# One operand moved to PSUM, sixteen gathers issued early, the tensor engine's edge loop written out, and the slots' stores issued by the scalar engine

## What is computed

```python
# L0, attention: softmax over a node's edges, weighted sum of h[src]
e = leaky_relu(a_src[src] + a_dst[dst], 0.2)
e = exp(e - segment_max(e, dst)[dst])
out = segment_sum((e / segment_sum(e, dst)[dst])[:, :, None] * h[src], dst)
x = layernorm(x + layernorm_affine(x + out @ proj_W.T))
# L1, twice: maximum over a node's edges
msg = x[src] @ W_msg + edge_attr @ W_edge
c = leaky_relu(segment_max(msg, dst) + x @ W_root + b)
# L2, twice: mean of h[src];  L3, three times: sum of h[src] * dis[src] * dis[dst]
```

## Time and profile before

| | us |
|---|---|
| median of 3 runs (8475.9 to 8486.47) | 8480.8 |
| the profiled execution, its own time | 8488.48 |
| its span | 8486.7 |
| POOL busy | 5071.0 (60%) |
| PE busy | 5045.5 (59%) |
| DVE busy | 4849.4 (57%) |
| ACT busy | 2773.5 (33%) |

### The profile page before, as it was taken

One profiled execution on the slowest core, in us unless ns is written; L12 is line 12 of the kernel. 1 busy time (PEld: TensorE's weight loads), 2 busy tenths in 40 slices (PEclk: granted clock), 3 DMA queues, 4 the chain that ended last, 5 costly groups with the idle time before them and its releaser, 6 DMA issues.

```text
span 8486.7 us, 103142 instructions
## 1 busy us (share of the span) xinstructions
PE 5045.5 (59%) x25358; PEld 3381.7 (40%) x25358; DVE 4849.4 (57%) x11584; ACT 2773.5 (33%) x4849; POOL 5071.0 (60%) x5030
## 2 busy tenths in 40 slices
PE   2100000000026887878786778877878598999998
PEld 1000000000013343433344434433434298999998
DVE  4654444444476666666666666666666676332234
ACT  0222222222214555555554455555555300000000
POOL 6777777777735777777777677777777600000000
PEclk6555555555556556555555555555555599999999
DMA  5232222222214444444443444444444365766766
GB/s 139 79 88 78 79 77 80 77 79 78 79 25 116 130 130 130 129 131 131 131 131 104 127 130 129 129 131 130 130 130 130 95 227 206 268 213 220 267 219 238
DMA packets 604993, 1132.63 MB, mean 133 GB/s; under 512 B 165186, under 2 KB 372437, under 8 KB 604328
## 3 DMA queue, kind: packets, MB, share of 16 engines
q1 hardware_dynamic: 407622, 678.22, 24.0%
q0 software_dynamic: 159184, 251.10, 14.2%
q10 hardware_dynamic: 37906, 200.73, 6.0%
HBM read 716.84 MB, written 412.70 MB: 133 GB/s over the span
## 4 chain that ended last, share of the span: by engine, by line
POOL 57%; PE 20%; issue 18%; DVE 3%; DMA 0%; ACT 0%; DVEq 0%; POOLq 0%; SPq 0%; ACTq 0%
POOL CG L466 55%; PE psB L721 6%; PE psX L721 6%; PE psA L721 6%; PE psO L653 2%; POOL ad_starts L440 1%; POOL EG L490 1%; PE psX L644 1%; PE psO L781 0%; DVE stat L1123 0%; DVE stat L1127 0%; DVE ARENA L1145 0%; DVE X L1125 0%; DVE EG L1126 0%; DMA ARENA<-ad_starts 0%
## 5 line engine op out<-in xcount | busy, mean ns | idle before, releaser
L466 POOL DMA_INDIRECT CG<-table,BUF x4704 | 4709.1, 1001 | 1615.9 <-issue 1433.0
L698 PE MATMUL psO<-WE,BUF 32*128 32x96 f32 x6272 | 1288.0, 385 | 95.3 <-issue 78.7
L698 PEld LDWEIGHTS psO<-WE,BUF 32*128 32x128 f32 x6272 | 1208.0, 291 | 229.0 <-issue 229.0
L764 PE MATMUL psA<-ident,F 128*100 128x128 f32 x1 | 0.5, 453 | 1895.8 <-DVEq L1347 1895.8
L1435 DVE TENSOR_SCALAR BUF<-iota,EG 128x392 bf16<-128x392 f16 x3136 | 1074.7, 343 | 0.0
L453 POOL CAST CG<-EG x35 | 26.0, 742 | 1315.2 <-DVEq L1118 1315.2
L1434 DVE TENSOR_SCALAR BUF<-iota,EG 128x128 bf16<-128x128 f16 x3136 | 772.2, 246 | 19.4 <-DMA EG<-step_rows 19.4
L764 PEld LDWEIGHTS psA<-ident,F 128*100 128x100 f32 x1 | 0.2, 160 | 1896.2 <-DVEq L1347 1896.2
L963 ACT COPY psX<-BUF 128x768 f32<-128x768 f32 x392 | 314.4, 802 | 1014.4 <-DVE STG L1449 493.1
L1443 DVE TENSOR_TENSOR STG<-CG,psO 128x768 f32<-128x768 f32 x196 | 288.5, 1472 | 601.2 <-DMA CG<-table,BUF 601.2
L1372 DVE TENSOR_TENSOR terms<-CG,ARENA 128x32 f32<-128x32 f32 x196 | 42.0, 214 | 1031.4 <-DMA CG<-table,BUF 1031.3
(11 more groups left out here) (276 smaller groups left out, 7866.8 us busy)
## 6 DMA issues: line engine op xcount, KB each, us to landing
BUF<-counts SPq DMA_DIRECT2D x245, 784.0 KB, 5.8
BUF<-counts ACTq DMA_DIRECT2D x245, 784.0 KB, 6.4
counts<-BUF SPq DMA_DIRECT2D x1572, 98.0 KB
hist<-CG SPq DMA_DIRECT2D x392, 384.0 KB
hist<-CG SPq DMA_DIRECT2D x196, 416.0 KB
CG<-table,BUF POOLq DMA_INDIRECT x4704
BUF<-in_edge_attr SPq DMA_DIRECT2D x392, 128.0 KB
table<-TB SPq DMA_DIRECT2D x14, 336.0 KB
```

Of the source, the lines that this page charges most:

```text
L466: pool.indirect_dma_start(out=rows_in[:, r, k, :], out_offset=None, in_=tab, in_offset=bass.IndirectOffsetOnAxis(ap=SRC[:, u * S + k:u * S ...
L698: mm = pe.matmul(ETERM[:, s, k // 4, (k % 4) * DIM:(k % 4 + 1) * DIM], EA[:, s, k, :], WE[:, n0 // ITERS, :], start=True, stop=True)
```

## The change

1. **Weights in PSUM.** `psB` is declared earlier, and `weights` is a view of it. ACT makes two exponentials a slot in place of one: the decays as before, and the weights into PSUM. DVE's product reads the weights there. ACT takes the exponentials of slot u after slot u - 1 has been scanned, for there is one weights tile.
2. **16 early gathers.** `gather_slot(0)` stands ahead of the scatters of the start, behind a wait for the stored table, and `gather_slot(1)` behind them, ahead of the wait for the reloaded values.
3. **PE's passes written out.** The hardware loop of `edge_terms` is straight code; PE waits once a slot for all four scaled identities (`keep_ready` now counts slots), ahead of the slot's first count matmul; one-hots count steps and not tiles (DVE increments `onehot_ready` once for each four).
4. **ACT issues the stores.** `store(u - 1)` stands right behind `rows_back(u - 1)` on ACT, in all three passes; SP has none.

```diff
--- before.py
+++ after.py
@@ -122,6 +121,8 @@
     psX = ctx.enter_context(nc.psum_tensor("psX", [P, 1024], F32))
+    psB = ctx.enter_context(nc.psum_tensor("psB", [P, 512], F32))
+    weights = psB[:, 0:HEADS * K9].rearrange("p (h k) -> p h k", h=HEADS)
     X = sb("X", [P, NB, DIM])
...
@@ -433,6 +434,17 @@
+        def gather_slot(u, tab, rows_in):
+            for k in range(S):
+                pool.indirect_dma_start(
+                    out=rows_in[:, u % RING, k, :], out_offset=None, in_=tab,
+                    in_offset=bass.IndirectOffsetOnAxis(ap=SRC[:, u * S + k:u * S + k + 1], axis=0)).then_inc(
+                        gathered[u % RING], 16)
+        pool.wait_ge(edges_loaded, EDGES_LOADED)
+        pool.wait_ge(table_stored, 16 * NG)
+        gather_slot(0, table0, ROWS0)
         pool.wait_ge(node_idx, 1)
@@ -440,6 +452,7 @@
                                     bounds_check=EPAD - 1, oob_is_err=False).then_inc(ad_scattered, 16)
+        gather_slot(1, table0, ROWS0)
         pool.wait_ge(ad_stored, 16)
@@ -458,23 +471,17 @@
-            for u in range(SLOTS):
+            for u in range(2 if q == 0 else 0, SLOTS):
                 r, lap = u % RING, q * LAPS + u // RING
...
                     pool.wait_ge(hist_stored[r], 16 * lap)
-                for k in range(S):
-                    pool.indirect_dma_start(
-                        out=rows_in[:, r, k, :], out_offset=None, in_=tab,
-                        in_offset=bass.IndirectOffsetOnAxis(ap=SRC[:, u * S + k:u * S + k + 1], axis=0)).then_inc(
-                            gathered[r], 16)
+                gather_slot(u, tab, rows_in)
...
-            if q == 0:
-                pool.wait_ge(edges_loaded, EDGES_LOADED)
             pool.wait_ge(table_stored, 16 * NG * (q + 1))
...
@@ -552,15 +554,9 @@
-            def store(u):
-                r, lap = u % RING, q * LAPS + u // RING
-                sp.wait_ge(block_done[r], lap + 1)
-                sp.dma_start(rec[:, u * S * width:(u + 1) * S * width], ring[:, r, :]).then_inc(hist_stored[r], 16)
             for u in range(SLOTS):
...
                     flush(u)
-                store(u)
                 if q in MAX_PASSES and u + 2 < SLOTS:
@@ -665,40 +661,28 @@
-        def count_steps(m, i, s):
-            for j in range(CS):
-                k = m * HALF + s * CS + j
-                sums = psM[j % 2][:, 0:CW]
-                pe.wait_ge(onehot_ready, i * (2 * HOTS) + (HOTS * (m * SLOTS + s) + 4 * j + 4))
-                pe.sem_inc(turn["pe"], 1)
-                pe.wait_ge(acc_ready, i * (2 * CS) + (k + 1))
-                pe.sem_inc(turn["pe"], 1)
-                pe.matmul(sums, LO[:, j, 0, :], RHS[:, j, 0, :], start=True, stop=False)
-                pe.matmul(sums, LO[:, j, 1, :], RHS[:, j, 1, :], start=False, stop=False)
-                pe.wait_ge(keep_ready, i * (2 * CS) + (k + 1))
-                pe.sem_inc(turn["pe"], 1)
-                pe.wait_ge(acc_ready, i * (2 * CS) + (k + 2))
-                pe.sem_inc(turn["pe"], 1)
-                pe.matmul(sums, KI[:, j, :], ACC[:, (j - 1) % CS, :], start=False, stop=True).then_inc(counted, 1)
         def edge_terms(q):
...
             m = MAX_PASSES.index(q)
-            n0 = m * ITERS
             pe.wait_ge(out_used, out_group_base({1: MAX1, 2: MAX2}[q], "carry") + 1)
-            with pe.Fori(0, ITERS) as i:
-                for s in range(2):
-                    pe.wait_ge(ea_loaded[s], i * 16 + 16 * (n0 + 1))
-                    pe.sem_inc(turn["pe"], 1)
-                    pe.wait_ge(eterm_used, i * 2 + (m * SLOTS + s + 1))
-                    pe.sem_inc(turn["pe"], 1)
-                    for k in range(S):
-                        mm = pe.matmul(ETERM[:, s, k // 4, (k % 4) * DIM:(k % 4 + 1) * DIM], EA[:, s, k, :],
-                                       WE[:, n0 // ITERS, :], start=True, stop=True)
-                    mm.then_inc(eterm_ready[s], 1)
-                    count_steps(m, i, s)
+            for u in range(SLOTS):
+                s = u % 2
+                pe.wait_ge(ea_loaded[s], 16 * (m * ITERS + u // 2 + 1))
+                pe.wait_ge(eterm_used, m * SLOTS + u + 1)
+                for k in range(S):
+                    mm = pe.matmul(ETERM[:, s, k // 4, (k % 4) * DIM:(k % 4 + 1) * DIM], EA[:, s, k, :],
+                                   WE[:, m, :], start=True, stop=True)
+                mm.then_inc(eterm_ready[s], 1)
+                pe.wait_ge(keep_ready, m * SLOTS + u + 1)
+                for j in range(CS):
+                    k = m * HALF + u * CS + j
+                    sums = psM[j % 2][:, 0:CW]
+                    pe.wait_ge(onehot_ready, k + 1)
+                    pe.wait_ge(acc_ready, k + 1)
+                    pe.matmul(sums, LO[:, j, 0, :], RHS[:, j, 0, :], start=True, stop=False)
+                    pe.matmul(sums, LO[:, j, 1, :], RHS[:, j, 1, :], start=False, stop=False)
+                    pe.wait_ge(acc_ready, k + 2)
+                    pe.matmul(sums, KI[:, j, :], ACC[:, (j - 1) % CS, :], start=False, stop=True).then_inc(counted, 1)
             pe.wait_ge(acc_ready, (m + 1) * HALF + 2)
@@ -912,8 +896,9 @@
             for j in range(CS):
-                nc.scalar.activation(KI[:, j, :], ident[:, :], ACT.Copy,
-                                     scale=STEP[:, 4, u * CS + j:u * CS + j + 1]).then_inc(keep_ready, 1)
+                keep = nc.scalar.activation(KI[:, j, :], ident[:, :], ACT.Copy,
+                                            scale=STEP[:, 4, u * CS + j:u * CS + j + 1])
+            keep.then_inc(keep_ready, 1)
             for j in range(CS):
...
@@ -928,23 +915,29 @@
                                state_cols[u % 2][:, :, 1:K9].rearrange("p c k -> p k c")).then_inc(block_done[u % RING], 1)
+            def store(u):
+                act.wait_ge(block_done[u % RING], u // RING + 1)
+                act.dma_start(stored_rows[:, u * S:(u + 1) * S, :], ROWS0[:, u % RING, :, :]).then_inc(hist_stored[u % RING], 16)
...
             for u in range(SLOTS):
+                if u:
+                    act.wait_ge(scanned, u)
                 act.wait_ge(exp_in, u + 1)
-                nc.scalar.activation(EX[:, u % 2, :, :, :], EX[:, u % 2, :, :, :], ACT.Exp).then_inc(exp_done, 1)
+                nc.scalar.activation(EX[:, u % 2, 0, :, :], EX[:, u % 2, 0, :, :], ACT.Exp).then_inc(scales_made, 1)
+                nc.scalar.activation(weights, EX[:, u % 2, 1, :, :], ACT.Exp).then_inc(exp_done, 1)
                 if u + 2 < SLOTS:
                     head_resets(u + 2)
-                if u:
-                    act.wait_ge(scanned, u)
-                act.wait_ge(exp_done, u + 1)
+                act.wait_ge(scales_made, u + 1)
                 nc.scalar.copy(scales[:, :, 1:K9].rearrange("p (h w) k -> p h w k", w=HW),
...
                     rows_back(u - 1)
+                    store(u - 1)
                 c = (u - 2 - COLUMNS_SLOT) // 3
...
@@ -966,6 +962,10 @@
                                max_cols[u % 2][:, :, 1:K9].rearrange("p c k -> p k c")).then_inc(block_done[u % RING], 1)
+            def store(u):
+                act.wait_ge(block_done[u % RING], q * LAPS + u // RING + 1)
+                act.dma_start(stored_rows[:, u * S:(u + 1) * S, :], ROWSW[:, u % RING, :, :]).then_inc(hist_stored[u % RING], 16)
@@ -976,9 +976,11 @@
                     rows_back(u - 1)
+                    store(u - 1)
                 count_steps(m, u)
...
             rows_back(SLOTS - 1)
+            store(SLOTS - 1)
@@ -1392,7 +1394,7 @@
                         ROWS0[:, r, :, 0:SW].rearrange("p k (h w) -> p h w k", w=HW),
-                        EX[:, b, 1, :, 1:K9].unsqueeze(2).broadcast_to([P, HEADS, HW, S]), ALU.mult))
+                        weights[:, :, 1:K9].unsqueeze(2).broadcast_to([P, HEADS, HW, S]), ALU.mult))
                 if u:
@@ -1431,8 +1433,9 @@
                     for a in range(2):
-                        ts(LO[:, j, a, :], iota16[:, 0:P], STEP[:, 2 + a, column], None, ALU.is_equal).then_inc(onehot_ready, 1)
-                        ts(RHS[:, j, a, :], iota16[:, :], STEP[:, a, column], None, ALU.is_equal).then_inc(onehot_ready, 1)
+                        ts(LO[:, j, a, :], iota16[:, 0:P], STEP[:, 2 + a, column], None, ALU.is_equal)
+                        hot = ts(RHS[:, j, a, :], iota16[:, :], STEP[:, a, column], None, ALU.is_equal)
+                    hot.then_inc(onehot_ready, 1)
                 if u:
...
```

11 lines of the change are left out of this document (4 added, 7 removed).

## The result

The changed kernel takes **8267.8 us** (median of 4 runs, 8261.0 to 8269.8), the kernel before 8480.8 in the same comparison: ratio 0.9747, 95% interval [0.973, 0.9764]. Forecast were 8304, range 8273 to 8335. The profiled execution took 8261.0 us with a span of 8259.2.

What follows compares the result with a forecast made beforehand. POOL's row of gathers was taken to bound all three passes. Terms -161 + 1 - 17 = -177 took the profiled 8488.5 to 8311.5; with the runs' median 7.7 lower, the forecast was 8304 us, range 8273 to 8335.

Steps and rivals of the forecast that it cites:

- Weights in PSUM, -161 + 1: Pass 0: gathers beside DVE's product fall from 1.82 to 0.94 us, -161 (ends -150 and -173); last slot's exponentials +1.
- Rival A: Pass 0: something accompanying the product, not the product itself, holds the gather, which stays at 1.82; 8465 us, chance 0.04.
- half of the 23: Pass 0, first 26 slots: table pieces may catch gathers freed from the product; gain between 0 and 23, taken as 11.
- Early gathers, -17: Start: 16 gathers issued early bring slot 2 forward from 224.41; -17 us, ends -14 and -19.
- Stores on ACT, 0, by the issue: All passes: ACT's store issue, 0.5 to 0.6 us, is hidden or lies off POOL's row; 0 us.
- rival C: Passes 1 and 2: ACT's store issue takes 6.50 us and the loop outlasts POOL's slots; 8608 us, chance 0.03.
- PE's passes, 0 by cover: Passes 1 and 2: last count sum comes 1.6 us later, covered by 0.9 us of slack before the scan's end; 0.
- theory C: Passes 1 and 2, formed after the measurement: PE's wait delays flushes, so the last gather lands sooner; 16 to 18 us each.
- passes 1 and 2 as 0: Passes 1 and 2: POOL's row of gathers was to stay as before, with no gain or loss in the sum.
- a fifth of the 84 us either way: Passes 1 and 2: allowance for small phase shifts under the one-hots, widening the range from 8290 and 8318 to 8273 and 8335.
- rival B: Passes 1 and 2: late count sums shift one-hots, stretching gathers; +120 us, so 8424, or down to 8220; chance 0.07.

Runs made afterwards that it cites:

- experiment 1: The kernel before with only the product's weights moved to PSUM, ACT's two exponentials behind the scan: 10,439.3 us, ratio 0.9994, on a chip where before takes 10,410.6.

## Why the forecast was right, and where it was wrong

- **Weights in PSUM, -161 + 1: right.** -170.3 and -167.7, inside the ends, and the cause is shown (experiment 1). Rival A, 8465, is out. The 10 us more are in the slots with a table piece, for which I had taken 11, half of the 23: from slot 2 to 25 the stretched time fell by 21 us, in the 170 others by 149. The Trainium skill, SBUF - State Buffer, "Who interferes with whom", infers that a `tensor_tensor` does not stall the making of DMA descriptors. The gather, a DMA that POOL issues, is held up all the same by one with two SBUF inputs: 1.82 against 0.94 us, by that operand. Whether it is held at its reading of the row numbers, which the section's other rule would cover, or at the writing of descriptors, no run tells. That other rule I had given without its condition: the section frees a DVE instruction with one SBUF input only outside DVE's 2-port performance modes, and names `tensor_scalar`, which the one-hots are, among those that can enter them. The one-hots have one SBUF input and do stretch gathers here, by up to 0.2 us in the means above; in which mode they run no trace shows.
- **Early gathers, -17: right**, -17.1 and -17.3, and 15 to 18 in the run with them alone. The first scatter came at 115.11 (forecast 114 to 116).
- **Stores on ACT, 0, by the issue: right in size, wrong in what else it moves.** ACT's issue takes 0.33, not 0.5; rival C, which needed 5, is out. But I had counted the store that SP loses, and not the DMA that stands behind it on SP's queue, the edge load, which now goes 2 us ahead of the store. Whether that moved anything is open.
- **PE's passes, 0 by cover: right.** The first count matmul follows the identities by 0.05, not 0.6; the last sum of a slot ends 1.4 us ahead of the scan's end, so the cover held, with more left than the 0.9 forecast. Whether this part moved the phase (theory C) is open.
- **The step that failed: passes 1 and 2 as 0, with "a fifth of the 84 us either way".** I had named the 84 us of stretched gathers and their dependence on phase, and then allowed 17 us. It was 35 and 12. Of that stretched time 54 us were in the 341 gathers of phase 0.15 to 0.25, and with one-hots 0.28 us earlier six in seven of them were gone; on the second chip, with one-hots 0.21 earlier, 304 of 340 still stood there and lost 31 us in place of 55. The range for such a term should have been nearly all of it, 70 us down and as much up. In rival B I had the mechanism and its ends, 8220 to 8424, which hold the result, but gave it 7 in 100 and tied it to a late count sum; the one-hots did not come late, they came earlier. That the second chip's time lies inside the range is luck of the same kind.

What is shown: the stretching differs by the phase and the pair, and its change accounts for the time by which passes 1 and 2 fell, on both chips. What moved the phase is open. The edge load's place is supported by a correlation within the kernel before, and four slots without that load speak against it; part 3, by the later flushes, stays possible. What makes five chips take 22 to 27% longer is open as well.

## What to carry to other kernels

Where one engine's row of short, equal instructions is the bound, price each held-up instruction by the operand kind of what runs beside it: an operand moved to PSUM gave 0.88 us a slot here. When a DMA leaves a queue, look at what stood behind it there, since that now starts earlier (here by some 3 us against the last gather), and price it as a term of its own. And where two periodic rows beat against each other, the time hangs on hundredths of a us: take the whole of the stretched time as the range, and measure on more than one chip before a per cent is believed.

## What the runs showed that I had not expected

- In the kernels before and changed, on the chips where POOL is the bound, a gather that starts 0.14 to 0.21 us behind a pair of one-hots loses 0.24 to 0.27 us if the pair is not the slot's first, and nothing if it is; at 0.00 to 0.10 it loses next to nothing, at 0.30 0.04.
- The same kernel on five chips takes 10,350 to 10,740 us and on another 8485. On the slower ones the gathers' own durations are the same (0.943 to 0.948 undisturbed) and a change may have another worth: the weights in PSUM 0 in place of 2%, PE's written-out passes 2.7 to 3.1% in place of none forecast, the stores on ACT 0.7% slower.
- The handover from ACT's last identity to PE's matmul takes 0.05 us.
